# A GNN layer's first self product and edge sums computed turned: weights or z0 held, rows of nodes moving

## The reference

```python
xn = layernorm(x)
deg_inv = 1 / maximum(segment_sum(ones, dst), 1)
def sage(h, W_self, W_neigh, b):
    mean = segment_sum(h[src], dst) * deg_inv[:, None]
    return h @ W_self + mean @ W_neigh + b
gnn = sage(relu(sage(xn, W_self0, W_neigh0, b0)), W_self1, W_neigh1, b1)
x = x + gnn + mix(xn)          # mix: linear attention with relu(q), relu(k)
x = x + ffn(layernorm(x))      # ffn: two quantized products of 1024 x 4096
```

## Time and profile before

| | us |
|---|---|
| median of 3 runs | 1293.63 (1293.49 to 1293.86) |
| the profiled execution | 1292.96 |
| its span, first to last instruction | 1290.8 |
| TensorE busy | 1285.8 |
| VectorE busy | 860.6 |
| ScalarE busy | 661.1 |
| GpSimd busy | 99.0 |

### The profile page before, as it was taken

One profiled execution on the slowest core, in us unless ns is written; L12 is line 12 of the kernel. 1 busy time (PEld: TensorE's weight loads), 2 busy tenths in 40 slices (PEclk: granted clock), 3 DMA queues, 4 the chain that ended last, 5 costly groups with the idle time before them and its releaser, 6 DMA issues.

```text
span 1290.8 us, 18843 instructions
## 1 busy us (share of the span) xinstructions
PE 1285.8 (100%) x6386; PEld 614.4 (48%) x6386; DVE 860.6 (67%) x1481; ACT 661.1 (51%) x904; POOL 99.0 (8%) x91
## 2 busy tenths in 40 slices
PE   9999999999999999999999999999999999999999
PEld 5454445555545444444444444444444444444444
DVE  6854452464577778985992664337887978786774
ACT  7766565456312336633441764446863377465460
POOL 0000000000000002100000010124540100000000
PEclk9999999999999999999999999999999999999999
DMA  9498987657235466725867899999949829732533
GB/s 358 147 272 264 294 260 215 222 210 254 90 115 196 156 206 226 220 76 180 277 236 253 182 252 222 260 334 286 305 149 358 281 63 297 188 62 78 131 64 99
DMA packets 203205, 269.10 MB, mean 208 GB/s; under 512 B 110576, under 2 KB 144112, under 8 KB 199536
## 3 DMA queue, kind: packets, MB, share of 16 engines
q1 hardware_dynamic: 191120, 260.12, 63.6%
q0 software_dynamic: 1440, 5.24, 2.2%
q10 hardware_dynamic: 10560, 2.62, 1.6%
HBM read 184.33 MB, written 57.67 MB: 187 GB/s over the span
## 4 chain that ended last, share of the span: by engine, by line
PE 98%; DVE 1%; DMA 0%; issue 0%; ACT 0%; DVEq 0%; ACTq 0%
PE ps L2399 39%; PE ps L2736 14%; PE ps L2695 13%; PE ps L2853 9%; PE ps L2816 9%; PE ps L2532 8%; PE ps L2601 3%; PE ps L2451 1%; PE ps L2542 1%; PE ps L2433 1%; DVE Zb L1469 0%; PE ps L2898 0%; DMA XIN<-in_x 0%; PE ps L2420 0%; DVE st L1433 0%
## 5 line engine op out<-in xcount | busy, mean ns | idle before, releaser
L2399 PE MATMUL ps<-S,XH 128*128 128x512 f16 x1440 | 316.7, 379 | 0.0
L2399 PEld LDWEIGHTS ps<-S,XH 128*128 128x128 f16 x1440 | 140.5, 98 | 163.8 <-issue 0.2
L2399 PE MATMUL ps<-S,Zb 128*128 128x512 f16 x480 | 106.7, 379 | 0.0
L2532 PE MATMUL ps<-XH,S 128*128 128x512 f16 (+1 forms) x576 | 102.6, 339 | 0.0
L2399 PE MATMUL ps<-Zb,XH 128*128 128x512 f16 x432 | 94.8, 379 | 0.0
L1081 ACT ACTIVATE AT<-ps 128x320 f16<-128x320 f32 x40 | 17.4, 434 | 139.7 <-PE ps L2399 139.7
L2695 PE MATMUL ps<-XH,AT 128*128 128x512 f16 x400 | 86.7, 379 | 0.0
L2695 PE MATMUL ps<-Zb,AT 128*128 128x512 f16 x400 | 86.5, 379 | 0.0
L1752 DVE TENSOR_SCALAR STREAM<-tables,keys 128x320 f16 x240 | 71.0, 296 | 22.3 <-PE ps L2601 13.6
L2532 PEld LDWEIGHTS ps<-XH,S 128*128 128x128 f16 x576 | 56.1, 98 | 45.7
L871 ACT ACTIVATE STREAM<-STREAM 128x1024 f32<-128x1024 f32 x64 | 66.8, 1044 | 14.7 <-DMA STREAM<-in_w1t 13.2
(11 more groups left out here) (332 smaller groups left out, 2017.0 us busy)
## 6 DMA issues: line engine op xcount, KB each, us to landing
STREAM<-in_w_all SPq DMA_DIRECT2D x48, 512.0 KB, 4.9
STREAM<-in_w1t SPq DMA_DIRECT2D x42, 512.0 KB, 5.2
STREAM<-in_w2t SPq DMA_DIRECT2D x28, 512.0 KB, 5.8
XIN<-in_x SPq DMA_DIRECT2D x20, 512.0 KB, 5.6
Zb<-in_w1t SPq DMA_DIRECT2D x14, 512.0 KB, 7.1
blocks_scratch<-S SPq DMA_DIRECT2D x4, 1792.0 KB, 8.5
blocks_scratch<-STREAM SPq DMA_DIRECT2D x4, 1792.0 KB, 8.6
S<-blocks_scratch SPq DMA_DIRECT2D x7, 1024.0 KB, 10.6
```

The lines of the kernel that those rows point to most:

```text
L2399: last = mm(acc[:, n * BANK:(n + 1) * BANK], left(l, kc), right(kc, r)[:, n * BANK:(n + 1) * BANK], start=(kc == 0 and i == 0), stop=(kc = ...
L2532: last = mm(ps[:, 3 * j * BANK + a:3 * j * BANK + b], Wq_s[:, kc, l, mc], XH[:, r, kc, a:b], start=(kc == 0 and l == 0 and r == 0), stop=( ...
```

## The change

The self product and the edge sums are computed with the other operand held. A unit u = 3c + q (12 units) stands for the features of blocks c and c + 4 (128 each, in two banks) and the nodes of column part q: 512, 512 or 226 (`LAST_COLS`, without the padding). The self product holds blocks of W_self0 and moves XH; the edge sums hold blocks of Z and move AT, which is laid out anew so that 512 targets of one source tile can be read in four pieces. A unit has 48 matmuls in the self product and 40 in the edge sums.

With features on the partitions, b0 is a column for each block (one more small DMA), the eviction is two `tensor_scalar` passes for a unit, and 1/max(deg, 1) is a row of 1280 on all partitions (`inv_deg`, in HL), made by six matmuls with a block of ones held (GpSimd writes the ones over `iota_s` when the counts are done), two clips, one reciprocal and a fill. `h_rows` has two passes (scale by `inv_deg`, add the self product). The high and low halves and the Strassen sums are written straight to their places in XH and `h_more`, and the 30 DMA transposes go. Units of the edge sums use the banks 2, 6 and 0 in turn, the last one bank 2. `PARTS`, `S0_QUADS`, `H_QUADS`, `SUMS_AT` and the places of the W_neigh0 chunks (`N0_AT`) are given anew for 12 units. P1 of pair 0 waits for the lows of unit 9. The inverse degrees come back as columns for the second layer by way of DRAM.

```diff
+COL_PARTS = 3
+UNITS = KC // 2 * COL_PARTS
+LAST_COLS = N - 2 * 512
-PARTS = [1] * 4 + [2] * 10 + [3] * 5 + [2]
+PARTS = [1] * 4 + [2] * 6 + [2, 2, 1, 3, 2, 1, 3, 3, 1, 3, 3, 1]
-SUMS_AT = {0: (0, 1), 7: (2,), 8: (3,)}
-DEG_AT = 7 * BANK
+SUMS_AT = {0: (0, 1), 8: (2,), 9: (3,)}
+N0_AT = (0, 1, 2, 3, 4, 6, 7, 8)
-        S0_QUADS = {0: 0, 1: 1, 2: 2, 3: 3, 4: 4, 5: 5, 8: 6}
-        H_QUADS = {t: EARLY_QUADS + t // 2 for t in range(1, NT - 4, 2)}
+        S0_QUADS = {0: 0, 1: 1, 3: 2, 4: 3, 5: 4, 6: 5, 9: 6}
+        H_QUADS = {1: EARLY_QUADS, 4: EARLY_QUADS + 1, 7: EARLY_QUADS + 2}
...
                 dve.wait_ge(S("s0_ps"), t + 1)
                 dve.wait_ge(S(f"rows_out{j}"), 8 * NT + 16 * (t // 2))
-                V.scalar_tensor_tensor(u_out[:, j, :], banks(4 * j), col("c_h"), b0s,
-                                       ALU.mult, ALU.add).then_inc(S("s0"), 1)
+                for n in range(2):
+                    V.tensor_scalar(in_unit(u_out[:, j, :], t)[:, n, :], in_unit(banks(4 * j), t)[:, n, :],
+                                    col("c_h"), col("b0")[:, c + 4 * n:c + 4 * n + 1], ALU.mult, ALU.add)\
+                        .then_inc(S("s0"), 1)
...
                 dve.wait_ge(S("deg_ps"), 1)
-                link(V.tensor_scalar(col("deg"), ps[:, DEG_AT:DEG_AT + 2 * NT].rearrange("p (t e) -> p t e", e=2)[:, :, 0],
-                                     1.0, None, ALU.max))
-                link(V.reciprocal(col("deg"), col("deg")))
-                times(col("tmp"), at("p", WN0), col("a_h"), 1.0 / (XW * Z0_SCALE))
-                link(V.tensor_scalar(col("deg_h"), col("deg"), col("tmp"), None, ALU.mult))
+                for j in range(2):
+                    dve.wait_ge(S(f"rows_out{j}"), 8 * NT + 8 * UNITS)
+                link(V.tensor_scalar(inv_deg[:, 0:D], banks(2), 1.0, None, ALU.max))
+                link(V.tensor_scalar(inv_deg[:, D:NP_], banks(7, cut=NP_ - D), 1.0, None, ALU.max))
+                link(V.reciprocal(inv_deg, inv_deg))
+                link(V.memset(h_small, 0.0))
+                times(col("c_deg"), at("p", WN0), col("a_h"), 1.0 / (XW * Z0_SCALE))
...
+            def h_rows(u):
+
+                j, T = u % 2, h_rows_of(u)[:, :, 0:unit_width(u)]
+                wide = inv_deg[:, unit_cols(u)].unsqueeze(1).broadcast_to([P, 2, unit_width(u)])
+                wait(dve, "h_sq", u - COL_PARTS + 1)
+                wait(dve, "h_hi", 4 * (u - COL_PARTS + 1))
+                wait(dve, "h_lo", 4 * (u - COL_PARTS + 1))
+                dve.wait_ge(S("g0_ps"), u + 1)
+                V.scalar_tensor_tensor(T, in_unit(banks(unit_bank(u)), u), col("c_deg"), wide, ALU.mult, ALU.mult)\
+                    .then_inc(S("h_t1"), 1)
+                dve.wait_ge(S(f"rows_in{j}"), 16 * (u // 2) + 16)
+                dve.wait_ge(S("h_t1"), 2 * u + 1)
+                V.tensor_tensor(T, T, in_unit(XIN[:, j, :], u), ALU.add).then_inc(S("h_t1"), 1)
...
+            for u in range(UNITS):
+                h_rows(u)
+                if u - 1 in H_QUADS:
+                    quad(H_QUADS[u - 1])
+                if u > 0 and u != UNITS - 2:
+                    h_lows(u - 1)
+                h_sums(u)
+                if u == UNITS - 3:
+                    h_lows(u)
...
+            def s0_pe(u):
+
+                c, _ = unit(u)
+                between = counts_between(NT + u)
+                acc, W = in_unit(banks(4 * (u % 2)), u), weight(S0)
+                wait(pe, "s0", 2 * (u - 1))
+                for kc in range(KC):
+                    counted = kc in between and between[kc]()
+                    for i, (l, r) in enumerate(((0, 0), (0, 1), (1, 0))):
+                        for n in range(2):
+                            last = mm(acc[:, n, :], W[:, kc, r, (c + 4 * n) * P:(c + 4 * n + 1) * P],
+                                      XH[:, l, kc, unit_cols(u)], start=(kc == 0 and i == 0),
+                                      stop=(kc == KC - 1 and i == 2))
...
-                for t in range(NT):
+                pe.wait_ge(S("iotas"), 4)
+                for to, at_, width in ((2 * BANK, 2 * P, BANK), (3 * BANK, 6 * P, BANK), (7 * BANK, 0, 2 * P)):
                     for n, part in enumerate((deg_hi, deg_lo)):
-                        last = mm(ps[:, DEG_AT + 2 * t:DEG_AT + 2 * t + 2], deg_part(part, t), one16[:, :],
-                                  start=(t == 0 and n == 0), stop=(n == 1), skip_group_check=True)
+                        last = mm(ps[:, to:to + width], iota_s, part[:, at_:at_ + width], start=(n == 0), stop=(n == 1))
...
+            def h_unit(u):
+
+                c, _ = unit(u)
+                acc = in_unit(banks(unit_bank(u)), u)
+                wait(pe, "h_t1", 2 * (u - 2 if u == UNITS - 1 else u - COL_PARTS) + 1)
+                for s in range(NT):
+                    if u == 0:
+                        z0_ready(s)
+                    for r in range(2):
+                        for n in range(2):
+                            last = mm(acc[:, n, :], Z[:, r, s, (c + 4 * n) * P:(c + 4 * n + 1) * P], AT_cols(u, s),
+                                      start=(s == 0 and r == 0), stop=(s == NT - 1 and r == 1))
```

More of the change, by code:

```diff
@@ L570, in _ @@
             late_mean(NT + 1)
-            for t in range(NT):
[L572 to L575, removed]
+            for t in range(UNITS):
+                if t in N0_AT[:KC - 2]:
+                    k = N0_AT.index(t)
+                    load_split(Wneigh0, k + 2, k % 2, 42 + k)
+                sp.wait_ge(S("s0"), 2 * t + 2)
+                sp.dma_start(in_unit(rows(s0_d, t), t), in_unit(u_out[:, t % 2, :], t))\
+                    .then_inc(S(f"rows_out{t % 2}"), 16)
                 if t - 1 in S0_QUADS:
@@ L1124, in _ @@
             act.wait_ge(S("w_scales"), 1)
-            for t in range(NT):
-                if t < KC:
-                    split_chunk(weight(S1), t, t % 2, 40 + t, at("s", WN0))
+            for t in range(UNITS):
+                if t in N0_AT:
+                    k = N0_AT.index(t)
+                    split_chunk(weight(S1), k, k % 2, 40 + k, at("s", WN0))
                 counts_act(NT + t)
@@ L1194, in _, with in_unit_dump @@
+            def in_unit_dump(u):
+                width = h_rows_of(u).shape[2]
+                return banks(4).rearrange("p (h n) -> p h n", h=2)[:, :, 0:width]
             act.wait_ge(S("prep_out0"), 16 * KC // 2)
             act.wait_ge(S("w_scales"), 2)
-            for p in range(PAIRS):
-                h_act(p)
-                for t in (2 * p, 2 * p + 1):
-                    if t in H_QUADS:
-                        for part in range(4):
-                            quad_round(H_QUADS[t], part)
+            for u in range(UNITS):
+                if u == UNITS - 1:
+                    act.wait_ge(S("c_x"), 1)
+                    st_copy(0, 0)
+                h_act(u)
+                if u in H_QUADS:
+                    for part in range(4):
+                        quad_round(H_QUADS[u], part)
@@ L1204, in z1_at @@
+            st_copy(0, 1)
+            st_copy(0, 2)
             def z1_at(r, t, half):
@@ L2647, in _ @@
                 u_pe(t)
-            def s0_pe(t):
-                wait(pe, "s0", t - 1)
-                product(banks(4 * (t % 2)), of_x(t), of(weight(S0)),
-                        between=counts_between(NT + t)).then_inc(S("s0_ps"), 1)
+            def s0_pe(u):
+                c, _ = unit(u)
+                between = counts_between(NT + u)
[8 more added lines that the diff above has]
+                                      stop=(kc == KC - 1 and i == 2))
+                            if counted and i == 0 and n == 0:
+                                last.then_inc(S("a_ps"), 1)
+                last.then_inc(S("s0_ps"), 1)
             pe.wait_ge(S("split_lo"), 40)
@@ L2658, in _ @@
             pe.wait_ge(S("u"), NT)
-            for t in range(1, NT):
-                s0_pe(t)
+            for u in range(1, UNITS):
+                s0_pe(u)
             def z0_pe(t):
```

272 lines of the change are left out of this document (136 added, 136 removed).

## The result

| | before | after |
|---|---|---|
| median, us | 1293.56 (1293.17 to 1293.86, 4 runs) | 1318.36 (1317.69 to 1319.51, 4 runs) |
| the profiled execution, its span | 1292.96, 1290.8 | 1318.16, 1316.1 |
| self product, start to start | 117.58 | 126.67 |
| edge sums, start to start | 86.33 | 94.65 |
| Strassen products, start to start | 181.57 | 183.54 |

What follows compares the result with a forecast made beforehand. TensorE, never idle from self product to edge sums, was taken as the bound. Columns -3.4, late counts +7.6 and inverse degrees +3.3 gave +7.5 us: 1301.1 us as a median, range 1294.6 to 1307.5 us.

Steps and rivals of the forecast that it cites:

- Columns: TensorE's matmul columns: self product -2.1 us, edge sums -1.8 us, degrees +0.6 us, in sum -3.4 us.
- the forecast figure: Degrees on TensorE: four matmuls of 512 and two of 256 take 1.08 us, +0.6 us.
- the first rival: Only the columns count, VectorE keeps ahead in the self product: 1290.2 us; chance 0.08.
- The counts: Self product: VectorE's pairs come late for TensorE, stalls of 4.2, 0.6, 2.4 and 0.4 us, sum +7.6 us.
- The inverse degrees: Ahead of edge unit 0: wide reciprocal of 7.7 us delays c_x by 9.4 us against 6.1 us cover, +3.3 us.
- The rival of eight steps an element: Wide reciprocal at eight steps an element, 10.8 us: stall of 6.4 instead of 3.3 us, 1304.2 us; chance 0.17.
- The clock: Rival: TensorE's clock falls to 1.2 GHz in the two long stalls, half of 7.5 us on top, 1304.9 us; chance 0.12.
- The two stalls of the forecast: TensorE's long waits: 4.2 us for pairs at self-product unit 3, 3.3 us for c_x ahead of edge unit 0.
- the rival's rule: Clock rival: half clock for as long as the stall lasted, so half the stall's length on top; chance 0.12.
- The h stage: Edge sums: VectorE's 20 us for three units fit in TensorE's 21.1 us, so covered, no cost.
- Nothing there is next in line to be late: H stage and start of the Strassen products: evictions, lows and moved block loads all covered, no cost.
- the forecast's own sign of being wrong: Wrong if TensorE shows no wait at the three named places, or if the first Strassen product waits for h.

Runs made afterwards that it cites:

- e1: Against after: quads of the self product moved off the part behind a narrow unit, most of them one unit later; 1307.07 us.
- e8: After with the edits of e1, e2 and e3, edge-sum quads one unit earlier, and the first Strassen copy ahead of unit 10's ScalarE work; 1290.51 us.
- e5: Against before: an unused fill and one unused reciprocal of 1280 added on VectorE ahead of the degrees; 1299.12 us.
- e6: Against before: an unused fill and two unused reciprocals of 1280 added on VectorE ahead of the degrees; 1307.12 us.
- e2: Against after: c_x made right after the two clips, the reciprocal of 1280 and the fill moved behind z0_lo(9); 1313.25 us.
- e3: Against after: VectorE's quad of an edge unit moved behind the lows and sums of that unit; 1310.7 us.

## Why the prediction was wrong in size, point by point

**Columns: right.** Without waits the self product takes 115.0 us (e1, e8) and the edge sums 84.5 us (689.49 to 774.02 in e8), as forecast; 226-row matmuls keep their 97 ns beside their weight loads. The degrees start at 679.59 us and take 1.07 us, the forecast figure within 0.01. e8 comes within 0.3 us of the first rival's time, 1290.2 us. That it is so close is in part luck: its trace has the columns' -3.4 us, 0.4 us gained in the self product by the late part of before, which the forecast did not have, and 1.1 us lost in the FFN. So the large waits were a matter of order, since the same work in another order has none of them.

**The counts: right in place and in mechanism.** From start to start TensorE lost 4.5 us at unit 3, 1.3 at unit 6, 2.3 at unit 7 and 0.3 at unit 9, in sum 8.4; the forecast had 4.2, 0.6, 2.4 and 0.4, in sum 7.6. The bound of the first came from rows of before and held to 0.2 us: the pair was ready at 505.1 us against 504.9. Two terms were missing: TensorE goes through a late part itself more slowly (0.81 and 0.71 us at a clock of 1.00, instead of 0.54; 0.6 us in all), and the clock (below).

**The inverse degrees: right.** The wait was 3.7 us against 3.3. The reciprocal of 1280 took 8.15 us against 7.7: the slope of 5.9 ns for an element, read from 1, 5 and 10 elements, is (8150 - 164) / 1279 = 6.2 ns in the wide one. The rival of eight steps an element, 10.8 us, is out. The Trainium skill (VectorE: DVE Perf Modes, "First, the fixed hardware budget") gives the repeat count of 8; the measured 6.2 ns is six times the 1.04 ns of a plain pass and not eight, and the measurement decides.

**The clock: a rival that should have been a term.** It was given a chance of 0.12 and a price of half the stall's length. Behind the three stalls of over 3 us it cost 2.6 us (12 matmuls at 4.71 instead of 2.59 us, and the late part at 1.03 instead of 0.54), 1.5 us (82.36 against 80.83 us) and 1.8 us (40 matmuls in 5.85 instead of 4.03 us). The two stalls of the forecast thus cost 4.1 us more than their waits, near the 3.75 us that the rival said, but by another rule, so that the nearness is luck: e5 and e6 show 1.7 and 2.2 us for 3.5 and 11.7 us of wait, where the rival's rule gives 1.8 and 5.9. The step that failed is the weight: "No stretch of this trace shows less than 1.00" was read as evidence against a fall, where TensorE of before has no stall in these stages that could have shown one. The Trainium skill (TensorE: Matmul & The Clock Gate, "What's actually happening") has an idle array fall to the lower level, and the traces agree (0.50).

**The h stage: the step that failed.** The forecast said "That fits, and three sets of banks give slack" from a sum of work, 20 us of VectorE in 21.1 us of TensorE. The sum came out to 0.1 us, but two errors cancel in it: the passes overlap a little, so the work is 18.2 us without GpSimd beside it, and GpSimd adds 1.8 us, which the forecast had priced in the counts and not here. And the sum is not the period: the two engines wait for each other inside a unit, and VectorE's list holds the quad, which waits for ScalarE, ahead of the sums, which ScalarE waits for. A step of order was taken in the count stage, where the recurrence was written out, and left out here; the period was 24.3 us against TensorE's 21.1. What it cost: 5.7 us ahead of unit 11, 0.7 and 1.8 us ahead of the Strassen products, and 1.8 us of clock, 10.1 us in all. "Nothing there is next in line to be late" was wrong for P1 and for its copy; the forecast's own sign of being wrong, that the first Strassen product waits for h, came true (0.7 us).

The sum of what was missing, in spans (25.3 us against 7.5): 0.8 in the counts' waits, 0.6 in the late parts themselves, 0.4 at c_x, 4.1 of clock behind those two, 10.1 in the h stage and 1.2 in the FFN; 0.6 us is spread over the other stages.

**Left open.** From the end of the Strassen products to the end of the span (the second layer's edge sums and the FFN) it is 332.6 us in after and 331.4 before, with the same matmuls. The edge sums are alike, so the FFN has the whole 1.2 us. e8 still has 1.1 us of it, and its waits at L2906 (the same code) are 0.6 and 0.3 us against 0.2 before. SyncE spends 10.90 us to issue three of its transposes there in e8 and 10.04 before. Whether that is the cause was not tried.

## What to carry to other kernels

When a loop runs over two engines that wait for each other, the sum of either one's work is only a lower bound of its period: write out one period in program order, with who waits for whom, and put that against the pace of the engine that sets the time. Work that is foreign to the loop, such as a block of weights prepared by the way, belongs behind the steps that the other engine waits for, and off the units that are short. In this kernel a TensorE stall of 3.5 us or more cost 1.5 to 2.8 us on top of its length.

## What the runs showed of the hardware that was not expected

- No fall of the clock stands behind the waits of 1.2, 1.8 and 2.1 us (1.00 in each stretch), and one stands behind each of those of 3.5, 3.7, 4.4, 5.7 and 11.7 us; no run has a wait between 2.1 and 3.5 us. TensorE's work then goes at half clock for some 3 to 6 us. When it falls differs between executions: behind the wait of 3.5 us only after TensorE is at work again, as the stretches of e5 show; in the wait of 11.7 us inside the wait, whose mean is 0.61. The wait of 4.4 us has 0.64 in its last 2.1 us in after and 0.98 in its last 3.0 us in e2.
- VectorE's reciprocal costs 6.2 ns for each element of a partition, six times a plain pass, and two of 1280 take twice one (16.34 and 8.15 us).
- VectorE's lows run slower where GpSimd has its part of the quad in hand (763.01 to 765.73 us in after): the two of 512 take 1.92 us instead of 1.02, that of 256 1.31 instead of 0.42. e3 takes GpSimd away from them, and the slowness goes with GpSimd. The lows are back at 1.02 and 0.42 us, and the pass of `h_rows` that adds two tiles (L2012), now beside GpSimd (762.22 to 763.31 us), takes 2.13 us instead of 1.23. The pass ahead of it (L2008, which reads PSUM) keeps its 1.28 us (760.88 to 762.16 us, with GpSimd at work from 761.04 to 762.13).
